# GpSimd's work in a GRU and transformer kernel: halved operations, other starting points, and two edits in the first time block

## The reference

```
x = x + GRU(h0 = cond_2048, inputs = x)          # 128 steps, one after the other
ada = cond @ ada_w + ada_b -> shift1, scale1, gate1, shift2, scale2, gate2
x1 = ln(x) * (1 + scale1) + shift1
q, k, v = x1 @ qkv_w + qkv_b                      # 16 heads of 128
attn_out = softmax(q k^T / sqrt(128)) v @ out_w + out_b
y = x + gate1 * attn_out
x2 = ln(y) * (1 + scale2) + shift2
y = y + gate2 * (gelu(x2 @ ffn_w1 + ffn_b1) @ ffn_w2 + ffn_b2)
out = x + y
```

## Time and profile before

| | |
|---|---|
| median of 3 runs | 790.56 us (790.0 to 791.43) |
| profiled execution, own time | 788.85 us |
| its span (first to last instruction) | 787.0 us |
| PE busy | 731.8 us (93%) |
| VectorE busy | 585.4 us (74%) |
| ScalarE busy | 483.4 us (61%) |
| GpSimd busy | 105.4 us (13%) |
| mean granted TensorE clock | 0.977 of full speed |

### The profile page before, as it was taken

The page is one execution under the profiler, slowest core; times in us unless marked ns, Lnnn a source line. Parts: engine busy times, 40 slices in busy tenths (PEclk is TensorE's granted clock), DMA queues, the critical chain, the costliest instruction groups (busy, mean ns, idle before and its releaser), DMA issues.

```text
span 787.0 us, 25437 instructions
## 1 busy us (share of the span) xinstructions
PE 731.8 (93%) x10488; PEld 532.9 (68%) x10488; DVE 585.4 (74%) x1586; ACT 483.4 (61%) x1633; POOL 105.4 (13%) x131
## 2 busy tenths in 40 slices
PE   5998899899988889999999999999989999999997
PEld 4777788788777676666667676666656666644545
DVE  4678877888878868777788886888877888744553
ACT  4345555555555557666677666876657766666453
POOL 0222232222322110000020010020010200100030
PEclk9779999999999989999999999999999999999999
DMA  6121112111121002222222222222222222210001
GB/s 225 43 95 45 43 44 80 47 43 43 46 74 37 3 15 42 45 41 46 48 35 48 42 41 43 42 41 42 42 42 41 42 42 42 41 28 27 23 6 53
DMA packets 77466, 36.71 MB, mean 47 GB/s; under 512 B 70395, under 2 KB 73639, under 8 KB 77223
## 3 DMA queue, kind: packets, MB, share of 16 engines
q1 hardware_dynamic: 76775, 33.52, 19.0%
q10 hardware_dynamic: 576, 1.57, 0.5%
HBM read 16.20 MB, written 2.10 MB: 23 GB/s over the span
## 4 chain that ended last, share of the span: by engine, by line
PE 68%; DVE 12%; ACT 10%; DMA 4%; issue 3%; SPq 1%; DVEq 0%; POOL 0%; ACTq 0%; POOLq 0%
PE bank L401 16%; PE bank L403 16%; PE bank L402 16%; PE bank L504 11%; PE bank L511 5%; DVE h_hi L1117 4%; ACT prob L918 3%; DMA pT_lo<-p_lo 3%; ACT zg L864 2%; ACT nu L867 2%; DVE prob L1209 2%; DVE mx L1192 1%; PE bank L421 1%; ACT p_hi L911 1%; DVE p_lo L1203 1%
## 5 line engine op out<-in xcount | busy, mean ns | idle before, releaser
L401 PE MATMUL bank<-y_hi,w_hi 128*128 128x512 f16 (+2 forms) x452 | 138.1, 318 | 0.9 <-DVE y_lo L1063 0.9
L402 PE MATMUL bank<-y_hi,w_lo 128*128 128x512 f16 (+2 forms) x452 | 138.1, 318 | 0.0
L403 PE MATMUL bank<-y_lo,w_hi 128*128 128x512 f16 (+2 forms) x452 | 138.1, 318 | 0.0
L504 PE MATMUL bank<-h_hi,whh_hi 128*128 128x16 f16 x1536 | 109.9, 173 | 26.8 <-DVE h_hi L1117 25.1
L504 PEld LDWEIGHTS bank<-h_hi,whh_hi 128*128 128x128 f16 x1536 | 89.0, 96 | 50.9 <-DVE h_hi L1117 46.9
L918 ACT ACTIVATE prob<-bank,nmx 128x128 f32<-128x128 f32 x256 | 90.4, 365 | 45.2 <-DVE nmx L1195 45.2
L504 PE MATMUL bank<-h_hi,whh_lo 128*128 128x16 f16 x1536 | 107.8, 172 | 0.0
L401 PE MATMUL bank<-w_hi,y_hi 128*128 128x128 f16 x512 | 90.3, 221 | 2.8 <-DVE v_lo L1199 2.8
L504 PEld LDWEIGHTS bank<-h_hi,whh_lo 128*128 128x128 f16 x1536 | 90.0, 97 | 0.6 <-issue 0.6
L402 PE MATMUL bank<-w_hi,y_lo 128*128 128x128 f16 x512 | 90.2, 221 | 0.0
L403 PE MATMUL bank<-w_lo,y_hi 128*128 128x128 f16 x512 | 90.2, 221 | 0.0
(11 more groups left out here) (157 smaller groups left out, 2158.4 us busy)
## 6 DMA issues: line engine op xcount, KB each, us to landing
stage<-in_weights SPq DMA_DIRECT2D x16, 640.0 KB, 3.8
x<-in_x SPq DMA_DIRECT2D x16, 128.0 KB, 3.8
out<-xr SPq DMA_DIRECT2D x3, 512.0 KB, 3.0
w<-in_ada_r SPq DMA_DIRECT2D x1, 1024.0 KB, 7.1
pT_hi<-p_hi SPq DMA_TRANSPOSE x64, 2.4
pT_lo<-p_lo SPq DMA_TRANSPOSE x64, 2.5
w<-in_W_ih ACTq DMA_DIRECT2D x2, 384.0 KB, 3.7
w<-in_W_hh ACTq DMA_DIRECT2D x2, 384.0 KB, 6.2
```

The costliest lines, as they stand in the source:

```text
L401: mm(ps, w[0], a[0], start=start, stop=False, skip_group_check=True)
L402: mm(ps, w[1], a[0], start=False, stop=False, skip_group_check=True)
L403: return mm(ps, w[0], a[1], start=False, stop=stop, skip_group_check=True)
L504: nc.tensor.matmul(out(m0 + m), half[:, k, w], h_hi[:, k * B:(k + 1) * B, 1], start=False, stop=False, skip_group_check=True)
```

## The change

GpSimd's operations in attention are cut in two (one for each of the two 128-feature halves, k = 0 and 1), so `norm_low` becomes two operations of 512 columns. Each operation of the groups 0 to 2 now also waits for a chosen value of `s_nm`, that is, for the scaled maximum of a chosen step: the two bias operations at first + 5 and + 6, the first sum at + 7, the second at + 9 and the two `norm_low` halves at + 14 and + 15, where first = 16 (g + 1) and `s_nm` stands at d after the maximum of step d - 1. The waits of other engines on `ln_lo` and `rest_ok` count twice as far.

In the GRU, `x_low` waits for one step more (`hlo_ok` t0 + 6, the `h_lo` of step s=4), and the second weight piece of a block for one step more (t0 + 7). In block 0 the four row modulation products and the two VectorE operations that take them up stand one step later, and `share_0` hands out the input products differently.

```diff
-ROW_TILES = {2: (0, 0), 3: (0, 1), 4: (1, 0), 5: (1, 1)}
+ROW_TILES = {3: (0, 0), 4: (0, 1), 5: (1, 0), 6: (1, 1)}
+REST_AT, LOW_AT = 5, 14
...
                 if r < NBL - 2:
-                    pool.wait_ge(hlo_ok, t0 + 5)
+                    pool.wait_ge(hlo_ok, t0 + 6)
                     x_low(r + 2)
-                piece_low(r * PB + 1, t0 + 6)
+                piece_low(r * PB + 1, t0 + 7)
...
-            def norm_low(g):
+            def behind_max(d):
+                pool.wait_ge(s_nm, d)
+            def norm_low(g, k):
                 pool.wait_ge(ln_hi, 2 * g + 2)
                 quad = slice(g * QUAD, (g + 1) * QUAD)
-                gtt(y_lo[:, :, quad, :].rearrange("p k j t -> p j k t"), yf[:, :, :, :],
-                    y_hi[:, :, quad, :].rearrange("p k j t -> p j k t"), sub).then_inc(ln_lo, 1)
+                gtt(y_lo[:, k, quad, :], yf[:, :, k, :], y_hi[:, k, quad, :], sub).then_inc(ln_lo, 1)
...
             for g in range(NG - 1):
-                sum_rest(g)
+                first = (g + 1) * H
+                for k in range(KD):
+                    behind_max(first + REST_AT + k)
+                    bias_rest(g, k)
+                behind_max(first + VAR - 1)
+                sum_rest(g, 0)
                 norm_rstd(g)
-                norm_low(g)
+                behind_max(first + VAR + 1)
+                sum_rest(g, 1)
+                for k in range(KD):
+                    behind_max(first + LOW_AT + k)
+                    norm_low(g, k)
...
-            share_0 = (0, 0, 0, 0, 6, 11, 16, 26, 36)
+            share_0 = (0, 0, 0, 8, 12, 16, 20, 26, 36)
...
-                    if r == 0 and s in (3, 5):
+                    if r == 0 and s in (4, 6):
                         row_modulation(s // 5)
```

More of the change, by code:

```diff
@@ L376, in sum_rest, with bias_rest @@
-            def sum_rest(g):
+                gtt(y_lo[:, k, quad, :], yf[:, :, k, :], y_hi[:, k, quad, :], sub).then_inc(ln_lo, 1)
+            def bias_rest(g, k):
                 quad = slice(g * QUAD, (g + 1) * QUAD)
                 pool.wait_ge(o_res, KD * (g + 1))
-                for k in range(KD):
-                    gtt(xr_v[:, k, quad, :, :], xr_v[:, k, quad, :, :],
-                        by_block(gb2[:, k, quad].unsqueeze(2).broadcast_to([P, QUAD, T])), add).then_inc(rest_a, 1)
-                pool.wait_ge(rest_a, g * KD + KD)
-                for k in range(KD):
-                    op = gtt(xr_v[:, k, quad, :, :], xr_v[:, k, quad, :, :], by_block(xr2[:, k, quad, :]), add)
-                op.then_inc(rest_ok, 1)
@@ L388, in _, with sum_rest @@
-            for g in range(NG - 1):
-                sum_rest(g)
-                norm_rstd(g)
-                norm_low(g)
-            norm_rstd(NG - 1)
-            norm_low(NG - 1)
-            sum_rest(NG - 1)
+                gtt(xr_v[:, k, quad, :, :], xr_v[:, k, quad, :, :],
+                    by_block(gb2[:, k, quad].unsqueeze(2).broadcast_to([P, QUAD, T])), add).then_inc(rest_a, 1)
+            def sum_rest(g, k):
+                quad = slice(g * QUAD, (g + 1) * QUAD)
+                pool.wait_ge(rest_a, g * KD + k + 1)
+                gtt(xr_v[:, k, quad, :, :], xr_v[:, k, quad, :, :], by_block(xr2[:, k, quad, :]), add
+                    ).then_inc(rest_ok, 1)
@@ new lines, in _ @@
+            for g in range(NG - 1):
+                first = (g + 1) * H
+                for k in range(KD):
+                    behind_max(first + REST_AT + k)
+                    bias_rest(g, k)
+                behind_max(first + VAR - 1)
+                sum_rest(g, 0)
+                norm_rstd(g)
+                behind_max(first + VAR + 1)
+                sum_rest(g, 1)
+                for k in range(KD):
+                    behind_max(first + LOW_AT + k)
+                    norm_low(g, k)
@@ L396, in _ @@
+            norm_rstd(NG - 1)
+            for k in range(KD):
+                norm_low(NG - 1, k)
+            for k in range(KD):
+                bias_rest(NG - 1, k)
+            for k in range(KD):
+                sum_rest(NG - 1, k)
         @block.tensor
@@ L560, in _ @@
                     if r == 0 and s in ROW_TILES:
-                        if s == 2:
+                        if s == 3:
                             pe.wait_ge(adaw_in, 32)
@@ L709, in up @@
                 if m == 0:
-                    pe.wait_ge(ln_lo, g + 1)
+                    pe.wait_ge(ln_lo, KD * (g + 1))
                 if t == 2:
@@ L1180, in norm_modulate @@
                 if g > 0:
-                    dve.wait_ge(ln_lo, g)
+                    dve.wait_ge(ln_lo, KD * g)
                 turned = bank[4] if g < NG - 1 else bank[6 + pair]
@@ L1240, in sum_group @@
                 dve.wait_ge(f_down, (g + 1) * FM + (seqs[0] // 2 if g == NG - 1 else 0))
-                dve.wait_ge(rest_ok, g + 1)
+                dve.wait_ge(rest_ok, KD * (g + 1))
                 for j in seqs:
```

## The result

The changed kernel takes 781.14 us (median of 4 runs, 779.88 to 783.30) against 790.28 (789.44 to 791.43) measured beside it: ratio 0.9886 [0.986, 0.9912], 9.0 us faster. In two later comparisons on other chips, of 6 runs each, the ratio was 0.9895 both times. The ratio of the two later comparisons, put on the forecast's 790.56 us, gives 782.3, which lies inside it: the miss is smaller than what separates one comparison from the next.

A forecast was written before the change was run, and what follows sets the result against it. The chain of waits was PE 68%, GpSimd 0%, so only stretched VectorE operations could pay. 3.24 + 3.5 + 0 + 0.2 = 6.9 us off the profiled 788.85 gave 781.9, or 783.6 from the median 790.56; range 781.4 to 786.4.

The forecast's parts named there:

- Term 1: GRU, blocks 2 to 13: `x_low` one step later ends one stretched `h_hi` per block, 12 x 0.27 = 3.24 us saved.
- the stall moves on to `nu`: GRU: the stall only moves to `nu` of step s=5, 786.8 us; chance 0.06.
- Term 2: Attention, groups 0 to 2: halves behind the maximum no longer hold up `nmx`, 3 x 1.17 = 3.5 us saved.
- Term 3: Attention: the sums no longer stretch `prob` and `nmx`; counted 0, upper end 2.2 us.
- `norm_scale` waits: Attention, head 9: `norm_scale` waits for the second sum, costing 1.7 us, 785.3 us; chance 0.10.
- Term 4: GRU, block 0 at half clock: input products handed out differently, 0.2 us saved, between -0.3 and +0.5.
- Transposes take over: Attention, short steps: PE waits for turned probabilities, two thirds of the `nmx` saving vanish, 785.9 us; chance 0.08.
- The clock helps as well: GRU, blocks 5 and 6: two clock falls of 0.74 us each vanish, 1.5 us more saved, 782.1 us; chance 0.14.

The follow-up runs named there:

- e6: The kernel before with `x_low` and the second weight piece each one step later: 782.97 us, ratio 0.993.
- e1: The kernel before with `x_low` alone one step later: 781.23 us, ratio 0.9905.
- e9: The changed kernel with `x_low` right behind the second weight piece, so that it meets `nu` of step s=7: 788.94 us, ratio 1.0006.
- e3: The kernel before with GpSimd's attention operations alone as in the changed kernel: 784.67 us, ratio 0.9948.
- e15: The changed kernel with the second sum of a group moved from first + 9 to first + 13: 780.72 us, ratio 0.9892.
- e2: The kernel before with the edits of block 0 alone: 788.51 us, ratio 0.9999.
- e8: The changed kernel with block 0 as before: 780.87 us, ratio 0.9894.
- e17: The changed kernel with unread matmuls in thin steps of blocks 0 to 13, except s=7 of blocks 5 to 13, and block 0's `x_high` behind s=3: 782.56 us.
- e18: The changed kernel with unread matmuls in blocks 0 and 1 alone and block 0's `x_high` behind s=3: 781.75 us, ratio 0.9909.
- e4: The changed kernel with `x_high` in block 0 behind step s=3 instead of s=1: 781.6 us, ratio 0.9901.
- e5: The changed kernel again, unedited, beside its variants on one chip: 780.9 us, ratio 0.9895.
- e16: The changed kernel again, unedited, on another comparison's chip: 781.42 us, ratio 0.9895.
- e13: The kernel before with six unread matmuls behind step s=4's products in blocks 2 to 13, stall kept: 787.17 us, ratio 0.9975.

## Why the prediction was wrong, step by step

- **Term 1** was right in its mechanism and, for blocks 2 to 13, in its size: no `h_hi` is stretched, `nu` stays clear, and 12 x 0.27 is what these blocks lost at full clock. It overlooked the thirteenth stall, because it looked at `h_hi` alone and said of block 1 that it has none: some 0.35 us more. e6 leaves 3.2 us, e1 4.5, for a forecast 3.24. The rival that the stall moves on to `nu` fell; e9 shows what it would have cost.
- **Term 2** was right: 1.14, 0.89 and 1.13 us by group against 1.17 each; e3 leaves 3.5 us for 3.5. A half takes 1.15 us, the 1.17 chosen, and `rden` comes behind it.
- **Term 3** counted 0 and found 0, though one reason was wrong. I had argued that `norm_scale`, running at the plain rate, wouldn't contend with the second sum. It does: 0.73 us for the pair became 1.25. The Trainium skill (SBUF — State Buffer, "Who interferes with whom") says that a `tensor_scalar` can enter a two-port mode and then contends with GpSimd. The trace agrees that it waits; the plain rate, 0.40 us for 256 columns, was no sign against it. No price shows: the step kept its 6.1 us, and e15, which removes the wait, is 0.7 us faster at the median, inside the intervals; so the rival `norm_scale` waits had the right event and the wrong price.
- **Term 4** was right for step s=4 of block 0, which lost 0.21 us for the 0.22 counted. The other parts can't be told from where the low clock lies in each execution, and e2 and e8 show no effect on the time. That block 1 begins earlier can't be read as its proof, since step s=2, with its wait for x, took from 2.0 to 3.2 us in different executions.
- **Transposes take over** didn't happen in the changed kernel (7.1 us of waits against 6.7 before), but the traces of e17 and e18 have 10.6 and 10.7 us of them and a longer attention, each in one execution.
- **The step that failed** is *The clock helps as well*. It was a rival with 0.14, priced at 1.5 us, and the sum counted nothing for it. Against it stood that "ten other blocks with the same stall kept the clock". That was read from one execution. Over three traces of kernels with the stall 9 of 36 blocks lost the clock right behind it, at changing places, and with it gone none does there. Over the eleven kernels with `x_low` moved and no fill, each execution has on average 8.4 us less low clock than before on its chip (1.4 us in e4 to 13.9 in e1), worth 1.4 us at 0.17 and 1.8 at 0.217. The price was near that; leaving it out of the sum was wrong. With it and block 1's 0.35 the sum of 6.9 us becomes 8.7 to 9.1, against 9.0 in the first comparison and 8.3 in the two later ones. Without the clock it is 7.3, against 6.2 to 6.7 left at fixed clock in e5 and e16, so the other terms came out a little smaller than counted, by what the means don't resolve.
- **The range** ended below at 781.4, with room for this one rival and 0.7 us beside it, where the upper end of term 4 gives only 0.3. What an execution varies by, about 0.2 us per us of low clock, had no room. That the first comparison fell 0.3 us outside and the two later ones inside is chance.

The Trainium skill (TensorE: Matmul & The Clock Gate, "The HAM clock gate") says that recent activity of the PE decides the clock, and that its phase differs from run to run. Both show here: e13 for the first, and for the second the falls past block 1, which the three traces of the changed kernel have in block 4 (the first), in block 14 (e5) and nowhere before the end of block 15 (e16).

## What to carry to other kernels

A stall on the ring of a latency-bound loop costs its own length and, where TensorE already has little to do in that step or the next, at times a fall of the clock as well; look at where the low stretches lie in several executions before calling them chance, and price them per us of low clock. In these traces an operation of GpSimd that reads SBUF held up five of VectorE's (`h_hi`, `nu`, `prob`, `nmx` and `norm_scale`), even the one of four numbers, until about its own end. Look at every operation of the ring for such a stretch, and not only at the one where it was first seen. Place GpSimd's operation behind the one that is on the path and ahead of a wait, or cut it in two. Ask of each such stretch whether its step has slack before counting it.

## What the hardware showed

- `nmx`, 4 columns, took 0.17 us alone and up to 1.33 beside a GpSimd operation; `norm_scale`, 256 columns, 0.40 alone and 0.94 beside one; `nu`, 32 columns, 0.19 and 0.68. `npre`, a scan with one input in PSUM, kept 0.28.
- Six matmuls of 128 columns per block, whose result is not used, made a kernel 0.25% faster (e13) by keeping TensorE at 2.4 GHz: a gap of 0.57 us in a step became 0.24, and the mean low clock 29.2 us where it was 39.6.
- Holding the clock in the first two blocks (e18) shortened blocks 0 to 2 by 1.2 us against e4, which has the same wait for x (47.98 against 49.15), for 17 us less low clock: 0.07 us per us and not 0.17 or 0.217. The low clock is cheap there; the runs don't show why. The "gain left" of the filled kernels is too low for that reason as well.
